# The second attention of a four-stage kernel: summary times W_out, scaled queries, and a new order of the tail

## The chip, the cores and the metric

One core of one Trainium2 chip. The metric is the device time of one execution in microseconds (us), as the median of several runs.

## The reference

One sequence of T = 2048 tokens with D = 128 features goes through four residual stages, each behind a layer norm: a causal softmax attention (16 heads of 8), a feed-forward with token shift, a linear attention, and the same feed-forward again.

```
x = x + attn_a(ln(x)); x = x + ffn(ln(x)); x = x + attn_b(ln(x)); x = x + ffn(ln(x))

attn_b: q, k, v = split(x @ w_qkv.T);  q, k = rope(q), rope(k)
        q_feat = elu(q * 8**-0.5) + 1;  k_feat = elu(k) + 1
        kv[h] = sum_t k_feat[t,h,:] outer v[t,h,:];  k_sum[h] = sum_t k_feat[t,h,:]
        out[t,h] = (q_feat[t,h] @ kv[h]) / max(q_feat[t,h] . k_sum[h], 1e-6)
        result = concat_h(out) @ w_out.T
ffn:    xr, xk = mixes of x[t] and x[t-1] by mu_r, mu_k
        result = sigmoid(xr @ W_r.T) * (square(relu(xk @ W_k.T)) @ W_v.T)
```

## The kernel before, in words

The tokens stand in four chunks (n = 0 to 3) of 512, each of four tiles of 128. Everything is fp32, in one program with a hand-written list of calls for each engine; an engine works its list strictly in order and waits at semaphores. A list entry such as `k_b(2)` is chunk 2 of that step; `(0, n)` and `(1, n)` are the first and second feed-forward, or queries (0) and keys (1) in `rope`, `features` and `feature_parts`.

Most of the span, up to 264 us, is the first attention: TensorE scores and weighs (L1126, L1147), ScalarE takes exponentials (L527). The change touches only what follows, the tail:

- First feed-forward: TensorE `mix_k_in` (L1201, L1205), `mix_r_in` and `mix_out` (both through `natural`, L980, four products of 128 columns in two passes each, so x8 in the trace); ScalarE `relu`, `squared`, `gate` (L542, L546, L551); VectorE `mix_r` (L864) and `add_mix` (L877, L878), which then takes the statistics of layer norm 3 (`ln_stats`, L652 to L658). `add_mix(0, n)` waits for both `gate(0, n)` and `mix_out(0, n)`. GpSimd raises the variance to -0.5 (`rstd_of`, L422) and forms the shift (L427); ScalarE applies the norm (`ln_act`, L536); TensorE turns it (`turn`, L975), ScalarE copies it out (L486).
- Second attention: TensorE `k_b`, `v_b`, `q_b` (L980). VectorE `rope` (L892 to L894, for chunk 3 also L898); for chunks 0 to 2 GpSimd adds the two halves (`turned`, L436). ScalarE `feature_parts` (L560, L561), VectorE `features` (L903). TensorE `summarize` (L1236) sums all chunks into `kv` and `k_sum` in one bank; VectorE `mask_kv` (L908, L909) keeps the blocks of the heads in `kvb[:, 0:D]` and puts `k_sum` by head in `kvb[:, D:D+H]`.
- Each chunk then passes `turn_q`, ScalarE's `turned_q`, `numerators` (L1250: numerators and denominators in one product of 144 columns), VectorE's `divide` (L915 maximum, L916 reciprocal, L917 product of the numerators in PSUM with the reciprocals), `turn_heads`, `turned_n`, `project_b` (L980, with W_OUT) and `add_y2` (L923 and the statistics of layer norm 4).
- Second feed-forward as the first, except that for chunks 1 to 3 VectorE forms both mixes (`mix_k_of` L870, L871; `mix_r` L864) after GpSimd's `shift` (L431). `add_mix(1, n)` ends a chunk and releases its store (L410).

The lists of TensorE, ScalarE and VectorE in the tail are the ones in the diff.

Of the kernel before, what the change touches and what calls it, by code (L numbers as in the profile page):

```python
# [18 lines left out]
P = 128  # L19
T = 2048  # L20
# [44 lines left out]
def program(nc, x_in, w_in, c_in, cb_in, krow_in, qrow_in, out):  # L65
    with ExitStack() as ctx:
# [62 lines left out]
        heads_out = mix_k  # L129
        k_tmp = att_t  # L130
        vb = scr[:, 14 * T + 8:14 * T + 8 + TILES * (D + 1)].rearrange("p (t n) -> p t n", t=TILES)
        kvb = scr[:, 15 * T + CH:15 * T + CH + D + H]
        w_mu = negmax[:, :].rearrange("p (i n) -> p i n", i=2)
# [45 lines left out]
        k_mixed = sem("k_mixed")  # L179
# [86 lines left out]
        def ln_apply(engine, waits, l, n, dst):  # L266
            waits.wait_ge(ln_rstd[l], n + 1)
            for j in range(TPC):
                ins = engine.tensor_scalar(dst[:, P * j:P * (j + 1)], x[:, TPC * n + j, :], negmean[:, n, j:j + 1],
                                           rstd[:, n, j:j + 1], ALU.add, ALU.mult)  # L270
            ins.then_inc(xh_ready[l] if l != LN1 else ln1_ready[n], 1)
# [143 lines left out]
        def _(pool):  # L415
# [54 lines left out]
            shift_of(LN4, 3)  # L470
            shift(1, 1)
            shift(1, 2)
            shift(1, 3)

        @block.scalar
        def _(act):
# [98 lines left out]

            relu(0, 0)
            squared(0, 0)
            gate(0, 0)
            relu(0, 1)
            squared(0, 1)  # L580
            gate(0, 1)
            ln_act(LN2, 3)
            relu(0, 2)
            squared(0, 2)
            turned_f(0, 3)
            gate(0, 2)
            ln_act(LN3, 0)
            ln_act(LN3, 1)
            relu(0, 3)
            squared(0, 3)  # L590
            gate(0, 3)
            turned_b(0)
# [4 lines left out]
            ln_act(LN3, 3)  # L597
            take_v(1)
            feature_parts(1, 0)
            turned_b(3)  # L600
            feature_parts(1, 1)
# [3 lines left out]
            feature_parts(1, 3)  # L605
            take_v(3)
            feature_parts(0, 1)
            feature_parts(0, 2)
            turned_q(0)
            turned_q(1)  # L610
            feature_parts(0, 3)
            turned_q(2)
            turned_n(0)
            turned_q(3)
# [8 lines left out]
            ln_act(LN4, 3)  # L623
            turned_f(1, 2)
            gate(1, 0)
            relu(1, 0)
            relu(1, 1)
            turned_f(1, 3)
            squared(1, 0)
# [7 lines left out]
            gate(1, 3)  # L637

        @block.vector
        def _(dve):  # L640
# [270 lines left out]
            def divide(n):  # L911
                dve.wait_ge(n_psum, n + 1)
                sums = ps[:, 2 * n:2 * n + 2, :].rearrange("p b (u m) -> p (b u) m", u=2)
                inv = rden[:, TPC * H * n:TPC * H * (n + 1)].rearrange("p (t h) -> p t h", h=H)
                then(nc.vector.tensor_scalar(inv, sums[:, :, D:D + H], 1e-6, None, ALU.max))  # L915
                then(nc.vector.reciprocal(inv, inv))  # L916
                nc.vector.tensor_tensor(heads_out[:, cols(n)].rearrange("p (t h v) -> p t h v", t=TPC, v=HD),  # L917
                                        sums[:, :, 0:D].rearrange("p t (h v) -> p t h v", v=HD),
                                        inv.unsqueeze(3).broadcast_to([P, TPC, H, HD]), ALU.mult).then_inc(n_ready, 1)
# [7 lines left out]

            add_y(3, high(3))
            add_mix(0, 0, LN3)
            add_mix(0, 1, LN3)  # L930
            mix_r(0, 3)
            add_mix(0, 2, LN3)
# [5 lines left out]
            features(1, 0)  # L938
            rope(0, 1)
            rope(1, 3)  # L940
            features(1, 1)
            features(1, 2)
            rope(0, 2)
            features(1, 3)
            features(0, 0)
            features(0, 1)
# [12 lines left out]
            mix_r(1, 0)  # L959
            mix_k_of(1)  # L960
            mix_r(1, 1)
            mix_k_of(2)
            mix_r(1, 2)
            mix_k_of(3)
            mix_r(1, 3)
# [3 lines left out]
            add_mix(1, 3, None)  # L969

        @block.tensor
        def _(pe):
# [273 lines left out]
            def numerators(n):  # L1246
                stage((kv_ready, 1), (qft_ready, max(n + 1, 2 * n - 2)))
                for j in range(TPC):
                    t = TPC * n + j
                    ins = nc.tensor.matmul(ps[:, t // 2, t % 2 * (CH // 2):t % 2 * (CH // 2) + D + H], qft[:, P * t:P * (t + 1)],  # L1250
                                           kvb[:, 0:D + H], start=True, stop=True)
                ins.then_inc(n_psum, 1)

            def turn_heads(n):
                pe.wait_ge(n_ready, n + 1)
                turn(heads_out[:, cols(n)], low(n, 1), nt_psum)

            def project_b(n):
                pe.wait_ge(nt_ready, n + 1)
                natural(high(n, 1), att_t[:, cols(n)], W_OUT).then_inc(y2_psum, 1)  # L1260

            def turn_ln4(n):
                stage((xh_ready[LN4], n + 1), (nt_ready, n + 1))
                turn(xh[:, cols(n)], low(n, 1), xt_psum[LN4])

            mix_k_in(0, 0)
            mix_r_in(0, 0)
            project(3)
            mix_out(0, 0)
            mix_k_in(0, 1)  # L1270
            mix_r_in(0, 1)
# [6 lines left out]
            turn_ln3(0)  # L1278
            mix_r_in(0, 3)
            turn_ln3(1)  # L1280
            mix_out(0, 3)
            k_b(0)
# [3 lines left out]
            q_b(0)  # L1286
            v_b(1)
            k_b(2)
            turn_ln3(3)
            q_b(1)  # L1290
            k_b(3)
            summarize(0)
            v_b(2)
            v_b(3)
            q_b(2)
            summarize(1)
            q_b(3)
            summarize(2)
            summarize(3)
            turn_q(0)  # L1300
            turn_q(1)
            numerators(0)
            turn_q(2)
            numerators(1)
            turn_heads(0)
            numerators(2)
            project_b(0)
            turn_q(3)
            turn_heads(1)
            numerators(3)  # L1310
# [9 lines left out]
            turn_ln4(2)  # L1320
            mix_k_in(1, 1)
            mix_r_in(1, 1)
            turn_ln4(3)
            mix_k_in(1, 2)
            mix_r_in(1, 2)
            mix_out(1, 0)
# [69 lines left out]
```

## Time and profile before

| | us |
|---|---|
| median of 3 runs (336.92 to 338.47) | 338.28 |
| profiled execution, its own time | 336.65 |
| profiled execution, span | 334.6 |
| TensorE busy in the span | 306.8 (92%) |
| ScalarE busy | 287.3 (86%) |
| VectorE busy | 161.4 (48%) |
| GpSimd busy | 57.6 (17%) |

The span lies within the execution's own time, which is 2.05 us longer. L numbers are lines of the kernel; PE is TensorE, PEld its weight loads, DVE VectorE, ACT ScalarE, POOL GpSimd. A merged entry such as "2.96 ... x2" is two instructions together.

### The profile page before, as it was taken

To read this page: it belongs to the slowest core of one execution; us is meant where nothing else is said; L and a number is where in the kernel's file an instruction comes from. 1 tells how busy PE (TensorE), PEld (TensorE's weight loads), DVE (VectorE), ACT (ScalarE), POOL (GpSimd) and SP (SyncE) were. 2 spreads that over 40 slices of the span, in tenths; PEclk is the share of its full clock that TensorE was granted. 3 is DMA by queue.
4 is the path that set the end of the run, shared out by engine and by line. 5 is a ranking of instruction groups with operands and counts; after the bars stand their busy time and mean duration, and the time that the engine had idled before them with its cause. 6 is when DMAs were issued, how large, how long until landed. Compare 5 with 4: busy or idle time off the path is not lost.

```text
span 334.6 us, 6057 instructions
## 1 busy us (share of the span) xinstructions
PE 306.8 (92%) x2314; PEld 132.5 (40%) x2314; DVE 161.4 (48%) x425; ACT 287.3 (86%) x411; POOL 57.6 (17%) x56
## 2 busy tenths in 40 slices
PE   3997999999999999999999999999999998979784
PEld 1562223233332323333332322223232467878564
DVE  6851133357545032432533313304613296998976
ACT  8547799998989999999889999998999678863782
POOL 5995000030000000100000100000000042910550
PEclk9996799999999999999999999999999999999999
DMA  7455566832004000000000000000000000000004
GB/s 222 141 150 184 164 187 190 243 123 76 0 2 125 3 0 2 0 2 0 2 1 3 0 2 0 2 0 2 0 3 0 2 0 3 0 2 0 2 1 125
DMA packets 13264, 16.43 MB, mean 49 GB/s; under 512 B 1488, under 2 KB 8016, under 8 KB 13136
## 3 DMA queue, kind: packets, MB, share of 16 engines
q1 hardware_dynamic: 13232, 16.01, 15.8%
q8 instruction: 20, 0.33, 0.4%
q14 instruction: 12, 0.10, 0.1%
HBM read 6.56 MB, written 2.62 MB: 27 GB/s over the span
## 4 chain that ended last, share of the span: by engine, by line
ACT 34%; PE 31%; DVE 17%; issue 12%; DMA 3%; SPq 1%; POOL 1%; ACTq 0%; DVEq 0%
ACT probs L527 23%; PE ps L1147 15%; PE ps L1126 11%; ACT parts_last L527 5%; ACT x L527 4%; PE ps L980 4%; DVE stats L652 3%; DMA kr<-parts_mid 2%; DVE scr L903 2%; DVE scr L892 1%; DMA x<-in_x 1%; ACT scr L536 1%; POOL rstd L422 1%; DVE mv L655 1%; DVE x L878 1%
## 5 line engine op out<-in xcount | busy, mean ns | idle before, releaser
L527 ACT ACTIVATE probs<-ps 128x1024 f32<-128x1024 f32 (+5 forms) x223 | 169.5, 859 | 13.2 <-PE ps L1126 12.1
L1126 PE MATMUL ps<-qr,kr 64*128 64x512 f32 (+6 forms) x592 | 110.7, 427 | 7.9 <-ACT probs L527 4.8
L1126 PEld LDWEIGHTS ps<-qr,kr 64*128 64x128 f32 x592 | 50.0, 187 | 125.8 <-ACT probs L527 85.8
L1147 PE MATMUL ps<-probs,vaug 128*9 128x512 f32 (+5 forms) x892 | 98.5, 499 | 0.4 <-DVE probs L845 0.4
L845 DVE TENSOR_TENSOR probs<-probs,cs 128x512 f32<-128x512 f32 x60 | 41.3, 689 | 99.9 <-ACT probs L527 99.7
L422 POOL TENSOR_TENSOR rstd<-veps,neghalf 128x4 f32<-128x4 f32 x16 | 17.1, 1068 | 222.7 <-DVE veps L658 222.6
L527 ACT ACTIVATE parts_last<-ps 128x1024 f32<-128x1024 f32 (+9 forms) x49 | 45.0, 974 | 1.4 <-PE ps L1126 1.2
L980 PE MATMUL ps<-w,scr 128*128 128x128 f32 x288 | 37.1, 280 | 2.6 <-DVE scr L864 1.1
L980 PEld LDWEIGHTS ps<-w,scr 128*128 128x128 f32 x288 | 34.4, 191 | 7.9 <-DVE scr L864 2.4
L1147 PE MATMUL ps<-parts_last,vaug 128*9 128x512 f32 (+9 forms) x196 | 25.4, 549 | 0.0
L1147 PEld LDWEIGHTS ps<-probs,vaug 128*9 128x9 f32 x892 | 13.6, 88 | 28.2 <-issue 17.1
L527 ACT ACTIVATE x<-ps 128x1024 f32<-128x1024 f32 (+4 forms) x24 | 20.5, 907 | 0.3 <-PE ps L1126 0.2
L779 DVE STREAM_TRANSPOSE ot<-ps 128x512 f32<-128x512 f32 x16 | 11.5, 717 | 16.8 <-PE ps L1147 16.5
L536 ACT ACTIVATE scr<-x,shift_by,rstd 128x128 f32<-128x128 f32 x36 | 14.8, 483 | 5.0 <-POOL shift_by L427 4.9
L975 PE MATMUL ps<-cs,scr 128*128 128x128 f32 x80 | 12.4, 280 | 2.6 <-ACT scr L536 2.1
L486 ACT COPY scr<-ps 128x512 f32<-128x512 f32 x17 | 9.7, 579 | 5.8 <-PE ps L975 5.6
L652 DVE BATCH_NORM_STATS2 stats<-x 128x6 f32<-128x128 f32 x64 | 13.9, 281 | 1.3 <-DMA x<-in_x 0.8
L1147 PE MATMUL ps<-x,vaug 128*9 128x512 f32 (+4 forms) x96 | 12.1, 566 | 0.0
L804 DVE TENSOR_TENSOR x<-ps,x 128x512 f32<-128x512 f32 x4 | 2.8, 692 | 19.0 <-PE ps L980 19.0
L975 PEld LDWEIGHTS ps<-cs,scr 128*128 128x128 f32 x80 | 8.8, 141 | 6.1 <-ACT scr L536 4.4
L446 POOL MEMSET qr<- 128x4096 f32 x3 | 10.5, 3506 | 0.0
L451 POOL MEMSET kr<- 128x4096 f32 x1 | 3.5, 3518 | 36.5 <-DMA kr<-parts_mid 36.5
(108 smaller groups left out, 238.5 us busy)
## 6 DMA issues: line engine op xcount, KB each, us to landing
x<-in_x SPq DMA_DIRECT2D x8, 256.0 KB, 3.9
qr<-parts_mid SPq DMA_DIRECT2D x16, 128.0 KB, 3.1
kr<-parts_mid SPq DMA_DIRECT2D x16, 128.0 KB, 3.1
kr<-att SPq DMA_DIRECT2D x8, 128.0 KB, 3.1
qr<-att SPq DMA_DIRECT2D x8, 128.0 KB, 3.2
qr<-parts_last SPq DMA_DIRECT2D x8, 128.0 KB, 3.7
kr<-parts_last SPq DMA_DIRECT2D x8, 128.0 KB, 3.2
out_y<-x SPq DMA_DIRECT2D x4, 256.0 KB, 2.3
```

The costliest lines, as they stand in the source:

```text
L422: nc.gpsimd.tensor_tensor(rstd[:, n], veps[:, n], neghalf[:], ALU.pow).then_inc(ln_rstd[l], 1)
L446: nc.gpsimd.memset(z.bitcast(F32)[:, :, :], 0.0).then_inc(zeroed, 1)
L486: nc.scalar.copy(dst, ps[:, bank, :]).then_inc(ready, 1)
L527: nc.scalar.activation(slot[:, 2 * u:2 * u + 2, w0:w1], ps[:, b:b + 2, w0:w1], ACT.Exp).then_inc(exp_done, 1)
L536: ins = nc.scalar.activation(xh[:, P * t:P * (t + 1)], x[:, t, :], ACT.Identity, bias=shift_by[:, n, j:j + 1], scale=rstd[:, n, j:j + 1])
L652: nc.vector.bn_stats(stats[:, n, j, :], x[:, TPC * n + j, :]).then_inc(dve_step, 1)
L779: nc.vector.transpose(ot[:], ps[:, 6 + ends[k].lane, :]).then_inc(ot_ready, 1)
L845: nc.vector.tensor_tensor(slot, slot, cs[:, C_TRI:C_TRI + P].unsqueeze(1).broadcast_to([P, 4, P]), ALU.min).then_inc(mask_done, 1)
L975: ins = nc.tensor.transpose(ps[:, bank, P * j:P * (j + 1)], src[:, P * j:P * (j + 1)], ident)
L980: ins = nc.tensor.matmul(ps[:, bank, P * j:P * (j + 1)], src[:, P * j:P * (j + 1)], w[:, c0:c0 + D], start=True, stop=True)
L1126: ins = nc.tensor.matmul(ps[:, 2 * (n % 3) + v, w0:w1], kr[kb // TPC][a:a + SIDE, j, P * (kb % TPC):P * (kb % TPC + 1)], qr[unit.c][a:a + ...
L1147: ins = nc.tensor.matmul(ps[32 * v:32 * v + V1, 6 + unit.lane, w0:w1], vaug[:, kb, V1 * h:V1 * (h + 1)], probs_slot(unit)[:, v, w0:w1], st ...
```

## The change

In the second attention the masked summary is turned (`turn_kv`), copied by ScalarE (`turned_kv`), multiplied by W_OUT (`kv_by_out`) and copied again (`take_kv_out`), once. TensorE forms only denominators from the turned features (`denominators`, 16 columns instead of 144). `divide` scales the queries' features in place, in SBUF, by the reciprocals; `turn_heads` turns these scaled features and `project_b` multiplies them by the copied product. A second edit moves the last layer-norm application (LN4, chunk 3) from ScalarE to VectorE (`ln4_last`, in `ln_apply`, L269), so that GpSimd forms no shift for it. The third is a new order of the lists of TensorE, ScalarE and VectorE in the whole tail. TensorE's wait for the last exponential moves from `mix_k_in(0, 0)` ahead of the first product of the list.

```diff
         q_rot, q_exp, q_relu, q_feat = prev_r, prev_k, mix_rt, mix_k
-        heads_out = mix_k
...
         kvb = scr[:, 15 * T + CH:15 * T + CH + D + H]
+        kv_turned, kv_out = (scr[:, 15 * T + 2 * CH + D * i:15 * T + 2 * CH + D * (i + 1)] for i in range(2))
...
-            ins.then_inc(xh_ready[l] if l != LN1 else ln1_ready[n], 1)
+            ins.then_inc(xh_last if (l, n) == (LN4, NCH - 1) else xh_ready[l] if l != LN1 else ln1_ready[n], 1)
...
             shift_of(LN4, 2)
-            shift_of(LN4, 3)
+            rstd_of(LN4, 3)
             shift(1, 1)
             shift(1, 2)
             shift(1, 3)
...
+            def turned_kv():
+                act.wait_ge(kvt_psum, 1)
+                nc.scalar.copy(kv_turned, ps[:, high(0, 1), 0:D]).then_inc(kvt_ready, 1)
+            def take_kv_out():
+                act.wait_ge(kvo_psum, 1)
+                nc.scalar.copy(kv_out, ps[:, high(0, 1), D:2 * D]).then_inc(kvo_ready, 1)
+            gate(0, 0)
+            gate(0, 1)
             relu(0, 0)
             squared(0, 0)
-            gate(0, 0)
             relu(0, 1)
             squared(0, 1)
-            gate(0, 1)
+            relu(0, 2)
             ln_act(LN2, 3)
-            relu(0, 2)
             squared(0, 2)
+            gate(0, 2)
             turned_f(0, 3)
-            gate(0, 2)
             ln_act(LN3, 0)
-            ln_act(LN3, 1)
             relu(0, 3)
             squared(0, 3)
+            turned_b(0)
+            ln_act(LN3, 1)
             gate(0, 3)
-            turned_b(0)
             ln_act(LN3, 2)
             turned_b(1)
             take_v(0)
             turned_b(2)
             ln_act(LN3, 3)
+            feature_parts(1, 0)
             take_v(1)
-            feature_parts(1, 0)
+            feature_parts(1, 1)
             turned_b(3)
-            feature_parts(1, 1)
             feature_parts(0, 0)
             feature_parts(1, 2)
             take_v(2)
-            feature_parts(1, 3)
             take_v(3)
             feature_parts(0, 1)
+            turned_q(0)
+            feature_parts(1, 3)
             feature_parts(0, 2)
-            turned_q(0)
             turned_q(1)
             feature_parts(0, 3)
             turned_q(2)
+            turned_kv()
             turned_n(0)
+            take_kv_out()
             turned_q(3)
             turned_n(1)
             turned_n(2)
...
             ln_act(LN4, 2)
             turned_f(1, 1)
-            ln_act(LN4, 3)
+            relu(1, 0)
+            squared(1, 0)
             turned_f(1, 2)
+            turned_f(1, 3)
             gate(1, 0)
-            relu(1, 0)
             relu(1, 1)
-            turned_f(1, 3)
-            squared(1, 0)
             squared(1, 1)
             gate(1, 1)
             gate(1, 2)
...
             def divide(n):
                 dve.wait_ge(n_psum, n + 1)
-                sums = ps[:, 2 * n:2 * n + 2, :].rearrange("p b (u m) -> p (b u) m", u=2)
-                inv = rden[:, TPC * H * n:TPC * H * (n + 1)].rearrange("p (t h) -> p t h", h=H)
-                then(nc.vector.tensor_scalar(inv, sums[:, :, D:D + H], 1e-6, None, ALU.max))
+                inv = rden[:, TPC * H * n:TPC * H * (n + 1)]
+                then(nc.vector.tensor_scalar(inv, ps[:, low(n, 1), 0:TPC * H], 1e-6, None, ALU.max))
                 then(nc.vector.reciprocal(inv, inv))
-                nc.vector.tensor_tensor(heads_out[:, cols(n)].rearrange("p (t h v) -> p t h v", t=TPC, v=HD),
-                                        sums[:, :, 0:D].rearrange("p t (h v) -> p t h v", v=HD),
-                                        inv.unsqueeze(3).broadcast_to([P, TPC, H, HD]), ALU.mult).then_inc(n_ready, 1)
+                q = q_feat[:, cols(n)].rearrange("p (t h v) -> p t h v", t=TPC, v=HD)
+                nc.vector.tensor_tensor(q, q, inv.rearrange("p (t h) -> p t h", h=H).unsqueeze(3).broadcast_to([P, TPC, H, HD]),
+                                        ALU.mult).then_inc(n_ready, 1)
...
+            def ln4_last():
+                ln_apply(nc.vector, dve, LN4, NCH - 1, xh[:, cols(NCH - 1)])
             add_y(3, high(3))
             add_mix(0, 0, LN3)
...
+            add_mix(0, 2, LN3)
             mix_r(0, 3)
-            add_mix(0, 2, LN3)
             add_mix(0, 3, LN3)
             rope(1, 0)
             rope(1, 1)
             rope(0, 0)
             rope(1, 2)
             features(1, 0)
+            features(1, 1)
             rope(0, 1)
+            features(0, 0)
             rope(1, 3)
-            features(1, 1)
             features(1, 2)
             rope(0, 2)
+            features(0, 1)
             features(1, 3)
-            features(0, 0)
-            features(0, 1)
             rope(0, 3)
             mask_kv()
             features(0, 2)
...
             mix_r(1, 0)
+            ln4_last()
             mix_k_of(1)
             mix_r(1, 1)
+            mix_r(1, 2)
             mix_k_of(2)
-            mix_r(1, 2)
+            mix_r(1, 3)
             mix_k_of(3)
-            mix_r(1, 3)
             add_mix(1, 0, None)
             add_mix(1, 1, None)
             add_mix(1, 2, None)
             add_mix(1, 3, None)
...
-            def numerators(n):
+            def turn_kv():
+                pe.wait_ge(kv_ready, 1)
+                nc.tensor.transpose(ps[:, high(0, 1), 0:D], kvb[:, 0:D], ident).then_inc(kvt_psum, 1)
+            def kv_by_out():
+                pe.wait_ge(kvt_ready, 1)
+                nc.tensor.matmul(ps[:, high(0, 1), D:2 * D], kv_turned, w[:, W_OUT:W_OUT + D], start=True, stop=True).then_inc(kvo_psum, 1)
+            def denominators(n):
                 stage((kv_ready, 1), (qft_ready, max(n + 1, 2 * n - 2)))
                 for j in range(TPC):
-                    t = TPC * n + j
-                    ins = nc.tensor.matmul(ps[:, t // 2, t % 2 * (CH // 2):t % 2 * (CH // 2) + D + H], qft[:, P * t:P * (t + 1)],
-                                           kvb[:, 0:D + H], start=True, stop=True)
+                    ins = nc.tensor.matmul(ps[:, low(n, 1), H * j:H * (j + 1)], qft[:, CH * n + P * j:CH * n + P * (j + 1)],
+                                           kvb[:, D:D + H], start=True, stop=True)
                 ins.then_inc(n_psum, 1)
             def turn_heads(n):
                 pe.wait_ge(n_ready, n + 1)
-                turn(heads_out[:, cols(n)], low(n, 1), nt_psum)
+                turn(q_feat[:, cols(n)], low(n, 1), nt_psum)
             def project_b(n):
                 pe.wait_ge(nt_ready, n + 1)
-                natural(high(n, 1), att_t[:, cols(n)], W_OUT).then_inc(y2_psum, 1)
+                pe.wait_ge(kvo_ready, 1)
+                for j in range(TPC):
+                    ins = nc.tensor.matmul(ps[:, high(n, 1), P * j:P * (j + 1)], att_t[:, CH * n + P * j:CH * n + P * (j + 1)], kv_out,
+                                           start=True, stop=True)
+                ins.then_inc(y2_psum, 1)
             def turn_ln4(n):
-                stage((xh_ready[LN4], n + 1), (nt_ready, n + 1))
+                stage((xh_last, 1) if n == NCH - 1 else (xh_ready[LN4], n + 1), (nt_ready, n + 1))
                 turn(xh[:, cols(n)], low(n, 1), xt_psum[LN4])
+            pe.wait_ge(exp_done, 3 + STEPS)
+            mix_r_in(0, 0)
+            mix_r_in(0, 1)
             mix_k_in(0, 0)
-            mix_r_in(0, 0)
...
+            mix_k_in(0, 1)
             mix_out(0, 0)
-            mix_k_in(0, 1)
-            mix_r_in(0, 1)
             mix_k_in(0, 2)
             mix_out(0, 1)
             mix_r_in(0, 2)
...
             mix_out(0, 2)
             mix_k_in(0, 3)
             turn_ln3(0)
+            mix_out(0, 3)
             mix_r_in(0, 3)
+            k_b(0)
             turn_ln3(1)
-            mix_out(0, 3)
-            k_b(0)
             v_b(0)
             turn_ln3(2)
             k_b(1)
             q_b(0)
+            k_b(2)
             v_b(1)
-            k_b(2)
+            v_b(2)
             turn_ln3(3)
             q_b(1)
+            summarize(0)
             k_b(3)
-            summarize(0)
-            v_b(2)
             v_b(3)
+            turn_q(0)
             q_b(2)
+            q_b(3)
             summarize(1)
-            q_b(3)
             summarize(2)
+            turn_q(1)
             summarize(3)
-            turn_q(0)
-            turn_q(1)
-            numerators(0)
+            denominators(0)
+            denominators(1)
             turn_q(2)
-            numerators(1)
+            turn_kv()
             turn_heads(0)
-            numerators(2)
+            kv_by_out()
+            denominators(2)
+            turn_q(3)
             project_b(0)
-            turn_q(3)
             turn_heads(1)
-            numerators(3)
+            denominators(3)
             turn_heads(2)
             project_b(1)
             project_b(2)
...
             turn_ln4(1)
             mix_r_in(1, 0)
             turn_ln4(2)
+            turn_ln4(3)
+            mix_out(1, 0)
             mix_k_in(1, 1)
             mix_r_in(1, 1)
-            turn_ln4(3)
+            mix_r_in(1, 2)
             mix_k_in(1, 2)
-            mix_r_in(1, 2)
-            mix_out(1, 0)
             mix_out(1, 1)
             mix_k_in(1, 3)
             mix_out(1, 2)
```

## Rows read from the trace of the kernel before

**Rows 1.** Busy time by stretch (start:end, length, busy us and instructions, clock)

```profile
0.00:264.00 264.00, 248.72 (x1899) 83.81 (x1899) 102.25 (x250) 239.86 (x314) 32.50 (x27) 0.98 0.19 58
...
290.00:300.00 10.00, 9.23 (x78) 8.51 (x76) 9.93 (x20) 7.97 (x15) 4.06 (x3) 1.00 0.01 2
...
325.00:330.00 5.00, 5.00 (x41) 4.52 (x40) 4.38 (x7) 3.41 (x6) 0.00 (x0) 1.00 0.22 67
```

**Rows 2.** Chain of waits that ended last (start us, us, what)

```profile
261.26 2.84 PE ps L1147 x24
...
266.26 1.17 PE ps L980 x8
...
269.68 0.60 DVE scr L877
...
272.46 0.60 DVE scr L877
...
300.99 1.26 PE ps L1250 x8
...
302.27 0.23 DVE rden L915
...
307.30 0.61 DVE x L923
...
317.03 0.07 issue
...
326.85 0.86 PE ps L1201 x2
327.71 2.69 PE ps L980 x24
...
331.22 0.69 DVE x L878
```

**Rows 3.** Timeline of ScalarE and VectorE around the first feed-forward's end

```profile
277.35 1.65 ACT L536 ACTIVATE scr<-x,shift_by,rstd 128x128 f32<-128x128 f32 x4 [0.97 <-POOL shift_by L427]
...
280.04 0.58 ACT L551 ACTIVATE scr<-ps 128x512 f32<-128x512 f32 x1
...
281.45 0.69 DVE L877 SCALAR_TENSOR_TENSOR scr<-scr,ps 128x512 f32<-128x512 f32 x1 [2.74 <-PE ps L980]
```

**Rows 4.** GpSimd's adds and VectorE's `features`, all (ns min/median/max), then the timeline

```profile
L436 POOL TENSOR_TENSOR scr<-scr x6: 1269/1276/1700, 285.7 to 295.8; 128x512 f32<-128x512 f32 x6
...
L903 DVE SCALAR_TENSOR_TENSOR scr<-scr x8: 679/685/1757, 289.3 to 303.7; 128x512 f32<-128x512 f32 x8
...
288.18 2.96 POOL L436 TENSOR_TENSOR scr<-scr 128x512 f32<-128x512 f32 x2
...
295.80 1.64 POOL L436 TENSOR_TENSOR scr<-scr 128x512 f32<-128x512 f32 x1 [3.17 <-DVE scr L894]
...
296.23 2.36 DVE L903 SCALAR_TENSOR_TENSOR scr<-scr 128x512 f32<-128x512 f32 x2
```

**Rows 5.** Timeline of TensorE's weight loads, and a large operand beside a small GpSimd instruction

```profile
290.30 0.97 PEld L1236 LDWEIGHTS ps<-scr 128*128 128x128 f32 x8
...
269.76 1.01 POOL L422 TENSOR_TENSOR rstd<-veps,neghalf 128x4 f32<-128x4 f32 x1 [79.22 <-DVE veps L658]
...
270.31 0.69 DVE L878 TENSOR_TENSOR x<-x,scr 128x512 f32<-128x512 f32 x1
```

**Rows 6.** Last layer norm and mixes: timeline, ns min/median/max, groups (busy us, mean ns | idle)

```profile
317.10 1.44 POOL L422 TENSOR_TENSOR rstd<-veps,neghalf 128x4 f32<-128x4 f32 x1 [0.77 <-DVE veps L658]
...
L871 DVE SCALAR_TENSOR_TENSOR scr<-scr,w x3: 750/977/1061, 319.0 to 323.9; 128x512 f32<-128x512 f32 x3
...
L864 DVE SCALAR_TENSOR_TENSOR scr<-scr,w 128x512 f32<-128x512 f32 x5 | 3.7, 745 | 0.5 <-POOL scr L431 0.5
...
L870 DVE TENSOR_SCALAR scr<-scr,omu 128x512 f32<-128x512 f32 x3 | 1.4, 483 | 1.0 <-ACT scr L486 1.0
...
139.37 1.12 DVE L269 TENSOR_SCALAR scr<-x,negmean,rstd 128x128 f32<-128x128 f32 x4 [1.14 <-POOL rstd L422]
```

More of the change, by code:

```diff
@@ L178, in program @@
         rot_ready, rot_last, feat_act, feat_ready = ([sem(f"{s}_{m}") for m in "qk"] for s in ("rot_ready", "rot_last", "feat_act", "feat_ready"))
-        k_mixed = sem("k_mixed")
+        k_mixed, xh_last = sems("k_mixed xh_last")
+        kvt_psum, kvt_ready, kvo_psum, kvo_ready = sems("kvt_psum kvt_ready kvo_psum kvo_ready")
         n_psum, n_ready, nt_psum, nt_ready, y2_psum, y2_added = sems("n_psum n_ready nt_psum nt_ready y2_psum y2_added")
```

## The prediction

> **What bounds the kernel now.** I read the stretches first. Up to 264 us TensorE and ScalarE carry the first attention, and nothing of the change is in there [rows 1]. All that can move is the tail, 264 to 334.6 us. Then the chain of waits: from 269.68 to 317.03 us it stands on VectorE nearly throughout [rows 2], and VectorE is busy for 9.93 of the 10 us from 290 to 300 [rows 1]. It leaves VectorE in that part at two places: before the fourth `add_mix`, where VectorE sat idle for 2.74 us [rows 3], and at the first numerators, from the end of `mask_kv`, 0.05 ahead of 300.99, to the start of `divide(0)` at 302.27, 1.33 us [rows 2]. Behind 317.03 (the end of `add_y2(3)`, called D below) the chain passes the last layer norm, and TensorE is full from 325 to 330 [rows 1]; it ends in three `natural` steps of 2.69 us together and VectorE's `add_mix(1, 3)`, at 331.91 [rows 2]. What the change is worth is thus the sum of VectorE's idle time and work from 267 us to D, and of whichever of VectorE and TensorE is last behind D. TensorE or ScalarE work saved elsewhere is worth nothing by itself.
>
> Prices that recur: a `natural` step in a stream 2.69 / 3 = 0.90 us, alone 1.17; `mix_k_in` 0.86 in a stream [rows 2]; an `add_mix` with its statistics 272.46 - 269.68 = 2.78 [rows 2], without them 0.60 + 0.69 + 0.04 of gaps = 1.33 [rows 2].
>
> **1. Entry, up to the fourth `add_mix`.** TensorE's part of the attention ends at 264.1, with the next loads begun at 264.0; `project(3)` then waited for the attention's last heads and started at 266.26 [rows 2]. Now two `mix_r_in` and a `mix_k_in` stand ahead of `project(3)`: 264.0 + 0.95 + 0.9 + 0.86 = 266.7, plus about 1.1 = 267.8, against 266.26 + 1.17 = 267.43. So `add_y(3)` and the first `add_mix` are later by 0.35: 270.03. The wait moved ahead of the list costs nothing by itself, since the old first entry waited for the same exponential. `add_mix` 0 to 2 then follow without gap: 270.03 + 3 x 2.78 = 278.37. `mix_r(0, 3)`, formerly between the second and third, comes behind: + 0.70 = 279.07. TensorE's `mix_r_in(0, 3)` takes 1.17: 280.25. ScalarE's `gate(0, 3)` takes 0.58 [rows 3] and a semaphore 0.05: `add_mix(0, 3)` starts at 280.95, against 281.45 [rows 3]. The new list puts `relu(0, 3)` ahead of the 1.65 us `ln_act(LN3, 1)` which stood before it [rows 3], so `mix_out(0, 3)` is done near 279.0; but `add_mix` needs the gate too, and that is late next. **Term: -0.5.** Bounds: -2.4, if the gate were no obstacle (279.05), and +0.35.
>
> **2. `features` beside GpSimd's adds.** The adds take 1.27 us each, but one 1.70; `features` take 0.68, but one 1.76 [rows 4]. These are the same event: GpSimd's add was issued at 295.80, just behind a `features`, and ended at 297.44; the next `features`, whose inputs were long there, was issued at 296.23 and ended near 297.97 (two in 2.36 us) [rows 4]. So a VectorE instruction with two SBUF inputs does not run beside a GpSimd add, and loses 1.757 - 0.685 = 1.07 us. `rope` reads PSUM and one SBUF table, and ran beside these adds unharmed.
> Before, behind `features(1, 0)` came `rope(0, 1)`; now `features(1, 1)`. At that moment GpSimd holds its fourth add: the third and fourth fill 288.18 to 291.14 [rows 4], 0.42 us more than two of 1.27, which is the wait for `features(1, 0)`. Everything is 0.5 earlier now: `features(1, 0)` ends near 289.5, GpSimd's add (chunk 2 of the keys) has waited since 288.95 and runs until 290.64, and `features(1, 1)` (its ScalarE input is ready at about 289.5) ends at 290.64 + 0.54 = 291.2 where 290.1 was possible. The old wait of 1.07 at 296.23 stays: `features(1, 3)` now stands behind the last add instead of `features(0, 0)`. `features(0, 0)` starts right at the end of `rope(0, 1)`, some 0.1 us before GpSimd's next add is released, and goes first. **Term: +1.1.** Bounds: 0, if VectorE gets in ahead of the waiting add, and +2.2, if `features(0, 0)` is caught too.
> The Trainium skill ("SBUF — State Buffer", section "SBUF: two separate sides") says of this: VectorE with two SBUF inputs and GpSimd share a port pair, the first to start holds it, the other blocks fully. These rows agree for large operands. Read strictly, the rule also speaks against the new `divide`, whose product now has two SBUF inputs instead of PSUM and SBUF: `divide(3)` would meet the end of GpSimd's power on four elements, and the sum would rise by some 0.35. The rows show otherwise: `add_mix`'s second instruction (two SBUF inputs) took its usual 0.69 at 270.31 in the middle of such a power of 1.01 us [rows 5]. My sum has nothing for it.
>
> **3. The rest up to `mask_kv`.** TensorE's new order has `v_b(2)` ahead of `turn_ln3(3)` (0.9 later, at about 287.7), `turned_b(3)` ends at about 290.1 and `k_b(3)` at 291.6; VectorE needs it at 293.1. `q_b(3)` is done at 295.6, `summarize(3)` about 1 us behind `features(1, 3)`, beside `rope(0, 3)` of 2 us. ScalarE's feature parts stay at least 1 us ahead. **Term: 0**; without that cover `v_b(2)`'s 0.9 would count. `mask_kv` ends at 300.94 - 0.5 + 1.1 = 301.55.
>
> **4. The algebra.** Removed: four products of 144 columns, 1.26 us for a chunk [rows 2]. Added: four of 16 columns. No row shows one so narrow. From below, the weight loads bound it: eight loads of this size take 0.97 us [rows 5]; from above 1.26. I take 1.0, since the loads already fill most of the 1.26. Only the first chunk's is on the path: **-0.25** (0 to -0.3). The other three are hidden behind `divide`, of which the three instructions stay in number and size. Added once: a transpose, a product, two ScalarE copies of 128 columns, estimated at 1.2 us with their handovers from ScalarE's 0.58 us for 512 columns [rows 3] and a quarter of a `natural` step each, the rest being handovers. They lie beside `divide(0)`, `features(0, 3)` and `divide(1)`. From 301.55, `divide(0)` runs 302.55 to 304.05, `turn_heads(0)` and `kv_by_out` follow to 305.3, `denominators(2)` to 306.2, just when `divide(1)` ends (302.27 to 307.30 held `divide` 0 to 2 and `features(0, 3)`, 5.03 us [rows 2]). `turn_q(3)` and `project_b(0)` end at 307.65, against 307.58 for VectorE. So I add **+0.1**; if these two small waits do not coincide as I have them, 0 to +0.9. Then `divide(3)` and four `add_y2` follow as before, 9.73 us: D = 302.55 + 5.03 + 0.1 + 9.73 = 317.4, against 317.03.
>
> **5. Behind D.** Before, 331.91 - 317.03 = 14.88 us. GpSimd's power ends at D + 1.52 (1.44 us instead of 1.01, since it starts beside `mix_r`) [rows 6]; no shift behind it, no ScalarE 1.65. VectorE applies the norm in 1.12 [rows 6], pitch 1.08. Then VectorE has three `mix_k_of` (0.48 + 0.75 + gap = 1.27) and three `mix_r` (0.67 pitch) [rows 6], 5.82, four `add_mix` of 1.33 and 0.08 for the last. Sum 1.53 + 1.08 + 5.82 + 5.40 = 13.83. To this come three GpSimd `shift` instructions, which all read SBUF beside it: L871 took 0.75 to 1.06 [rows 6], so 0.31 at a hit; three hits make 0.85 to 0.9: 14.7. TensorE: `turn_ln4(3)` at D + 3.2, and then with waits for the mixes the last product ends near D + 13.05, + 1.46 = 14.5, so VectorE is last. **Term: -0.2.** Bounds: -1.0 (no hits) and +0.5 (each hit a whole `shift`, about 0.55).
>
> **Sum.** -0.5 + 1.1 - 0.25 + 0.1 - 0.2 = +0.2 on a span of 334.6 and an execution of 336.65. The stores behind the last `add_mix` stay. The profiled execution is 1.63 below the median of 338.28; I put the same change on the median: 338.5.
>
> **Rivals.**
> *Faster*: the collision at `features(1, 1)` does not come (a slightly earlier or later fourth add), and VectorE has no hits behind D: 0.2 - 1.1 - 0.8 = -1.7, 336.6. For it: the old trace shows only one such loss among six adds [rows 4]. Against: the fourth add was already waiting when `features(1, 0)` ran.
> *Slower*, one mechanism: VectorE loses against GpSimd wherever both want SBUF, at `features(0, 0)` too (+1.1), and for a whole `shift` at each of the three behind D (+0.7 over my term): 0.2 + 1.8 = +2.0, 340.3. It decides if GpSimd's add gets in ahead of `features(0, 0)`, that is, if that starts more than 0.1 us behind the end of `rope(0, 1)`; against it, its ScalarE input is 1.4 us early in my walk.
> *The change does not do what it says*: 16 columns cost as much as 144, and `kv_by_out` delays `project_b(0)`: +0.25 + 0.5, 339.2; no change that can be told.
>
> **How the numbers follow.** Forecast 0.50, its own range 337.6 to 339.4; faster rival 0.27; slower rival 0.17; the last 0.06. 0.5% is 1.7 us, about what a measurement can tell from no change. The faster rival stands on that border, as the bound of term 1 (-1.9 more) reaches beyond it, so its chance goes to faster; the forecast and the last go to same, 0.56. The range 336.4 to 340.0 leaves out about 1 in 10 at each side.
>
> **What would show it.** The fourth `add_mix` starts at 280.9 behind `gate` (not 279); one more L903 of about 1.7 us near 290; `mask_kv` ends near 301.5; denominators take 1.0; D near 317.4; no gap over 0.2 us ahead of `add_y2(0)`; L269 in some 1.1 to 1.6 us behind D, and VectorE without idle time from there to the end. I am wrong if the gate comes earlier, if `features(1, 1)` runs in 0.68, or if the end behind D is under 14 us.

## The result: slower, and the profile after

The changed kernel took 342.42 us (median of 4 runs, 341.72 to 345.63) against 337.64 for the kernel before in the same comparison: ratio 1.0157, 95% interval 1.0116 to 1.0198. I had forecast no change, 338.5, in a range of 336.4 to 340.0. Here and below, a ratio leaves out executions over 1.5% above the fastest of their kernel, so it is not the quotient of the medians.

Executions differ by some us before the attention ends, so all comparisons of traces below are of the *tail*: from the end of the attention's last 24 products to the end of the last `add_mix`. Tails and stretches are those of the profiled executions; of the others only the time and the mean clock are known. Before it was 331.91 - 264.10 = 67.81 us [rows 2]. In the changed kernel, the chain of waits (start, length, what):

```profile
261.62 2.80 PE ps L1163 x24
...
281.28 0.70 DVE scr L889
...
289.19 2.32 DVE scr L915 x2
...
301.90 3.38 PE ps L1274 x16
...
310.31 1.72 PE ps L1286 x8
312.03 0.02 issue
312.05 0.70 DVE x L934
...
321.88 0.07 issue
...
332.51 2.69 PE ps L996 x24
...
336.02 0.69 DVE x L890
```

The tail is 336.71 - 264.42 = 72.29 us, 4.48 longer. Up to the first denominators (L1274) it is 301.90 - 264.42 = 37.48, against 36.89 before [rows 2], and behind D (321.88) it is 14.83, against 14.88. Nearly all of the loss, 3.94 us, lies between: 19.98 against 16.04. There the chain, which stood on VectorE, stands on TensorE from 301.90 to 312.03. The stretches of the changed kernel show why (start:end, length; busy us of PE, PEld, DVE, ACT, POOL; then TensorE's granted clock):

```profile
298.00:301.90 3.90, 1.71 (x13) 1.28 (x13) 3.87 (x8) 2.00 (x4) 0.96 (x1) 1.00 0.00 0
302.10:312.30 10.20, 10.20 (x50) 10.02 (x50) 5.50 (x12) 2.75 (x7) 0.00 (x0) 0.50 0.01 2
```

Before, the same part of the kernel:

```profile
298.00:301.00 3.00, 1.27 (x9) 0.85 (x9) 2.96 (x8) 2.18 (x5) 0.00 (x0) 1.00 0.00 0
301.00:307.00 6.00, 5.79 (x48) 5.58 (x48) 5.05 (x11) 2.07 (x5) 0.00 (x0) 1.00 0.00 0
```

The granted clock went from 1.00 to 0.50 (2.4 to 1.2 GHz) at about 302.15, 0.25 us after the first 16-column product, and came back at about 312.4. TensorE is shown busy for the whole of it, the weight loads for 10.02 of 10.20 us, and yet it finished 50 matmuls in 10.2 us where before it finished 48 in 6. The timeline of the stretch:

```profile
301.90 3.38 PE L1274 MATMUL ps<-scr 128*128 128x16 f32 x16 [1.18 <-DVE scr L921]
...
303.61 0.23 DVE L926 TENSOR_SCALAR rden<-ps 128x64 f32<-128x64 f32 x1 [1.18 <-PE ps L1274]
...
309.41 0.23 DVE L926 TENSOR_SCALAR rden<-ps 128x64 f32<-128x64 f32 x1 [2.21 <-PE ps L1274]
...
312.05 0.69 DVE L934 TENSOR_TENSOR x<-ps,x 128x512 f32<-128x512 f32 x1 [1.10 <-PE ps L1286]
```

The first denominators took about 1.7 us (301.90 to 303.6), not 1.0; VectorE waited 2.21 us for the third chunk's and 1.10 us for the first `project_b`.

### The profile page after: what moved, and what is told of

Read it like the earlier page. It is cut to its first block, busy times and chain, and to the rows that moved or that the text cites. A ratio compares the mean times of both kernels' runs of the same rounds, so it can differ in the third digit from the quotient of the medians.

```text
span 339.8 us, 6068 instructions
## 1 busy us (share of the span) xinstructions
PE 310.4 (91%) x2317; PEld 137.7 (41%) x2317; DVE 164.2 (48%) x429; ACT 286.5 (84%) x409; POOL 57.0 (17%) x55
## 4 chain that ended last, share of the span: by engine, by line
PE 38%; ACT 34%; issue 12%; DVE 11%; DMA 3%; POOL 1%; SPq 0%; ACTq 0%; DVEq 0%
ACT probs L529 23%; PE ps L1163 14%; PE ps L1142 10%; PE ps L996 5%; ACT parts_last L529 5%; ACT x L529 4%; DMA kr<-parts_mid 2%; PE ps L991 2%; PE ps L1009 2%; DVE scr L915 2%; DVE stats L664 2%; PE ps L1274 1%; DVE scr L904 1%; PE ps L1217 1%; DMA cs<-in_consts 1%
## 5 line engine op out<-in xcount | busy, mean ns | idle before, releaser
L996 PE MATMUL ps<-w,scr 128*128 128x128 f32 x256 | 32.8, 279 | 2.4 <-DVE scr L876 1.1
L996 PEld LDWEIGHTS ps<-w,scr 128*128 128x128 f32 x256 | 30.6, 192 | 7.9 <-issue 3.1
L1163 PEld LDWEIGHTS ps<-probs,vaug 128*9 128x9 f32 x892 | 13.7, 89 | 28.0 <-issue 16.8
L991 PE MATMUL ps<-cs,scr 128*128 128x128 f32 x80 | 14.4, 309 | 3.8 <-ACT scr L538 2.1
L538 ACT ACTIVATE scr<-x,shift_by,rstd 128x128 f32<-128x128 f32 x32 | 13.2, 483 | 3.7 <-POOL shift_by L428 3.7
L991 PEld LDWEIGHTS ps<-cs,scr 128*128 128x128 f32 x80 | 10.6, 163 | 7.1 <-ACT scr L538 3.9
L1163 PE MATMUL ps<-x,vaug 128*9 128x512 f32 (+4 forms) x96 | 11.3, 529 | 0.0
L437 POOL TENSOR_TENSOR scr<-scr 128x512 f32<-128x512 f32 x6 | 8.8, 1470 | 4.7 <-DVE scr L906 4.7
```

The source lines that it names most:

```text
L538: ins = nc.scalar.activation(xh[:, P * t:P * (t + 1)], x[:, t, :], ACT.Identity, bias=shift_by[:, n, j:j + 1], scale=rstd[:, n, j:j + 1])
L991: ins = nc.tensor.transpose(ps[:, bank, P * j:P * (j + 1)], src[:, P * j:P * (j + 1)], ident)
L996: ins = nc.tensor.matmul(ps[:, bank, P * j:P * (j + 1)], src[:, P * j:P * (j + 1)], w[:, c0:c0 + D], start=True, stop=True)
L1163: ins = nc.tensor.matmul(ps[32 * v:32 * v + V1, 6 + unit.lane, w0:w1], vaug[:, kb, V1 * h:V1 * (h + 1)], probs_slot(unit)[:, v, w0:w1], st ...
```

## The experiments

Thirteen kernels were run. The lists moved in an edit are given by their entries.

**Which half of the change is it?** Four kernels together.

`e1_old_algebra`: the new lists, the old steps.

```diff
-            denominators(0)
+            numerators(0)
...
-            turn_kv()
...
-            kv_by_out()
```

> The changed kernel with all its new orders, but with the numerators of 144 columns, the division in PSUM and the projection by W_OUT of before. In the changed kernel TensorE's granted clock fell to 0.50 at about 302.2 us, 0.3 us after the first 16-column product, and came back at about 312.2. Theory IDLE (the thin work of TensorE between 297.9 and 301.9, a matter of the order, lets the clock fall): it falls here too near 302; the time is 340 to 342. Theory NARROW (products of 16 columns do it): the clock stays 1.00 and the time is that of before within 0.3%, 337 to 338.

Measured: 338.43 us (10 runs), ratio 1.0006 (0.9964 to 1.0048); tail 68.32 us, clock 1.00 in all of it.

`e2_algebra_alone`: the old lists, the new steps (the reverse diff, on the kernel before).

> The kernel before with the algebra alone: denominators, scaled queries, product with W_OUT once; all lists in the order of before, with the four small steps put in. IDLE: TensorE's work ahead of the denominators is that of before, the clock stays 1.00, the time is 337.5, within 0.3% of before. NARROW: the clock falls to 0.50 soon after the first denominators, the time is 340.5 to 342.5.

Measured: 342.12 us (4 runs), ratio 1.0143 (1.0071 to 1.0214); tail 72.43 us, clock 0.50 from 302.6 to about 316.3.

`e3_wide_denominators`: all of the change, but products of 128 columns, of which `divide` reads the last 16.

```diff
-                    ins = nc.tensor.matmul(ps[:, low(n, 1), H * j:H * (j + 1)], ...
-                                           kvb[:, D:D + H], start=True, stop=True)
+                    ins = nc.tensor.matmul(ps[:, low(n, 1), P * j:P * (j + 1)], ...
+                                           kvb[:, D + H - P:D + H], start=True, stop=True)
```

> The changed kernel with denominators of 128 columns in place of 16 (112 of them not used), each chunk in the same bank. IDLE: the clock falls near 302 all the same, since the work ahead of it is unchanged, and the time is 340.5 to 342.5. NARROW: the clock stays 1.00, the time is 337.5 to 338.5.

Measured: 338.12 us (10 runs), ratio 0.9999 (0.9962 to 1.0036); tail 68.31 us, clock 1.00.

`e4_filler`: all of the change, with two products added.

```diff
             turn_q(1)
+            nc.tensor.matmul(ps[:, 3, :], ident, w[:, 0:CH], start=True, stop=True)
             summarize(3)
+            nc.tensor.matmul(ps[:, 3, :], ident, w[:, 0:CH], start=True, stop=True)
             denominators(0)
```

> The changed kernel with two products of 512 columns added on TensorE, whose results nobody uses, one ahead of summarize(3) and one behind it, where TensorE waited for about 1.0 and 1.2 us. IDLE: the clock stays 1.00 and the time is 337.5 to 338.5. NARROW: the clock falls to 0.50 all the same, at most some us later, and the time is 340 to 342.5.

Measured: 338.30 us (10 runs), ratio 1.0012 (0.9969 to 1.0054); tail 68.18 us. Its stretches, which answer to the two of the changed kernel (its attention ended 3.57 us later):

```profile
301.50:305.40 3.90, 3.48 (x16) 1.82 (x16) 3.87 (x8) 1.94 (x4) 1.01 (x1) 1.00 0.00 0
305.50:312.00 6.50, 6.36 (x55) 5.95 (x55) 5.73 (x12) 2.95 (x8) 0.00 (x0) 1.00 0.00 0
```

What follows: the order alone costs nothing that can be told (e1), the algebra alone has the whole loss (e2), and it is neither the added steps nor the two added copies as such, since they run at full clock in e3 and, with the narrow products, in e4. Both of my theories are contradicted: IDLE by e1, e2 and e3, NARROW as I had put it by e4, where the narrow products are all there, at 1.08 us for the first chunk:

```profile
305.45 1.08 PE ps L1274 x8
```

**What sets the fall off, and what keeps it going?** The changed kernel with 128 columns for some chunks only (`m = P if n in (0,) else H`, and the reverse; `divide` reads the columns accordingly).

> The changed kernel, no filler, with the denominators of chunk 0 alone 128 columns wide, those of chunks 1 to 3 of 16. If the clock falls by how thin the work has been up to and just behind the start of the denominators, a wide first chunk keeps it at 1.00 and the time is 338 to 339. If each narrow product counts, the clock falls during chunk 1 and the time is 341 to 342.5.

Measured for `e7_wide_first`: 340.09 us (9 runs), ratio 1.0040 (0.9992 to 1.0088). The profiled execution kept its clock, tail 68.25. The time is outside both ranges that I gave. Two other executions had a mean clock of 0.975, where the lowest of e3's ten had 0.982, so they may have lost it; without their traces this stays open.

> The changed kernel, no filler, with the denominators of chunk 0 alone of 16 columns, those of chunks 1 to 3 of 128. If the first chunk decides, the clock falls near 302.2 us as in the changed kernel, but with wide products behind it comes back sooner than after 10 us; time 339.5 to 342. If the narrow products of chunks 1 to 3 are needed for the fall, the clock stays 1.00 and the time is 338 to 339.

Measured for `e8_narrow_first`: 340.06 us (9 runs), ratio 1.0046 (1.0007 to 1.0085). In the profile the clock fell at about 302.85, 0.25 us behind the first denominators, and was back at about 309.7, after 6.8 us in place of 10.2; tail 71.11. This is the first of the two cases that I gave.

Two later kernels were built for speed (below) and spoke to this as well. `e10_gate_alone` has the old algebra with its 144 columns, and in its profile the clock fell nevertheless, within 0.1 us of the start of the first numerators at 299.66:

```profile
296.00:299.70 3.70, 1.94 (x15) 1.33 (x13) 3.67 (x9) 2.73 (x5) 0.12 (x1) 1.00 0.02 4
299.70:303.10 3.40, 3.40 (x15) 3.39 (x16) 1.55 (x4) 1.01 (x3) 0.00 (x0) 0.50 0.00 0
303.10:305.00 1.90, 1.90 (x17) 1.90 (x17) 1.83 (x5) 0.84 (x2) 0.00 (x0) 1.00 0.00 0
```

So narrow products are not needed for a fall, but this one was over in 3.4 us. Nor does the work ahead decide alone: in the 3 us ahead of the first numerators TensorE was busy for 1.26 us in e10 and for 1.26 us before, and before it kept its clock. The fall was probably no rarity in e10: six of its twelve executions had a mean clock of 0.979 at 336.5 to 338.4 us, the profiled one among them, and in the kernel before a mean clock that low went with 340 us or more.

To tell the stretch ahead and the narrow products apart, 512-column products were put ahead of wide ones (`e12_gate_filler`) and behind narrow ones (`e13_filler_behind`: twice the filler line between `denominators(1)` and `turn_q(2)`).

> The kernel of e10 (the kernel before with the earlier gate, old algebra, products of 144 columns) with two unused products of 512 columns ahead of the first numerators, as in e9. In e10's profile the clock fell to 0.50 for about 3.4 us from 299.9, with wide products, and the tail was 67.36 us with numerators(0) at 2.29 in place of 1.26. Theory THIN (the fall is set off by the thin stretch ahead, the narrow products only keep it going): the filler holds the clock at 1.00, the tail is 66.2 to 66.7 us and the time 0.4% to 0.7% below before. If filler is no cover for wide products, the tail stays 67.3.

Measured: 336.67 us (12 runs), ratio 0.9965 (0.9937 to 0.9992), so 0.35% below before where I gave 0.4% at the least; clock 1.00 and tail 66.32, as THIN has it.

> The changed kernel, no filler ahead, but two unused products of 512 columns directly behind denominators(1). THIN: the fall at the first denominators comes all the same, since the work ahead of it is unchanged, but the clock is back after 3 to 6 us instead of 10.2, and the tail is 69.5 to 71.5 us against 72.29 in the changed kernel. If the narrow products set it off and keep it down whatever stands between, it stays down some 10 us and the tail is over 72.5.

Measured: 342.47 us (4 runs), ratio 1.0167 (1.0102 to 1.0232); tail 73.26. The clock fell 0.25 us behind the start of the first denominators and was back in the middle of the slice 308 to 309:

```profile
301.00:302.00 1.00, 0.59 (x4) 0.59 (x4) 0.95 (x4) 0.96 (x2) 0.00 (x0) 0.82 0.00 0
...
307.00:308.00 1.00, 1.00 (x2) 0.23 (x1) 0.00 (x0) 0.00 (x0) 0.00 (x0) 0.50 0.00 0
308.00:309.00 1.00, 1.00 (x8) 0.79 (x7) 0.00 (x0) 0.02 (x1) 0.00 (x0) 0.76 0.00 0
```

That is 6.8 us of low clock: less than the 10.2 of the change, but not the 3 to 6 that THIN gave. The tail is even longer than in the change and lies where I had put the rival (over 72.5), because the two fillers themselves ran at half clock on the path (3.6 us, from 304.8 to 308.4). So e13 bears neither theory out as written; with e8 it shows two falls with wider products behind the first narrow ones, both shorter than that of the change.

**Is the port collision worth undoing?** `e5_features_apart` is e4 with VectorE's list `features(1, 0)`, `rope(0, 1)`, `features(1, 1)`, `rope(1, 3)`, `features(0, 0)`, `features(1, 2)`.

> The kernel of e4_filler (the changed kernel with two unused products ahead of the denominators) with VectorE's list altered: rope(0, 1) between features(1, 0) and features(1, 1), and features(0, 0) behind rope(1, 3). The tail, from the end of the attention's last products to the end of the last add_mix, was 67.81 us before and 68.18 in e4. Theory PORT (features(1, 1) lost 1.1 us to GpSimd's add because it stood directly behind features(1, 0)): the L915 of about 1.7 us near features(1, 1) is gone, mask_kv ends 1.0 earlier and the tail is 67.1 to 67.3. Rival: the wait moves to another features or to k_b(3), and the tail stays within 0.3 of 68.18. In the time that is 0.3%, at the edge of what can be told.

Measured: 338.88 us (10 runs), ratio 1.0029 (0.9990 to 1.0067), tail 68.63, 0.45 longer than e4. The timeline of VectorE:

```profile
290.16 0.69 DVE L904 TENSOR_TENSOR scr<-ps,cs 128x512 f32<-128x512 f32 x1 [0.19 <-PE ps L996]
...
291.43 0.68 DVE L915 SCALAR_TENSOR_TENSOR scr<-scr 128x512 f32<-128x512 f32 x1
...
296.44 0.69 DVE L904 TENSOR_TENSOR scr<-ps,cs 128x512 f32<-128x512 f32 x1 [1.04 <-PE ps L996]
```

`features(1, 1)` runs in 0.68, so the loss at this place was indeed the collision. But `rope(0, 1)` now waits for `q_b(1)` (0.19 us by its row), and `rope(0, 2)` 1.04 us for `q_b(2)`, which stands behind `turn_q(0)` and so behind the moved `features(0, 0)`. The rival was right: the wait moved.

**Is the gate what the fourth `add_mix` waits for?** `e6_early_gate`: e5, and the entry altered. On ScalarE, not shown below, `gate(0, 3)` moves directly behind `squared(0, 3)`, and `turned_b(1)` ahead of `ln_act(LN3, 2)`.

```diff
+            mix_r(0, 3)
             add_mix(0, 2, LN3)
-            mix_r(0, 3)
...
             mix_k_in(0, 3)
+            mix_r_in(0, 3)
             turn_ln3(0)
             mix_out(0, 3)
-            mix_r_in(0, 3)
```

> The kernel of e5 with the entry altered: mix_r(0, 3) ahead of add_mix(0, 2) on VectorE, mix_r_in(0, 3) ahead of turn_ln3(0) on TensorE, gate(0, 3) directly behind squared(0, 3) and turned_b(1) ahead of ln_act(LN3, 2) on ScalarE. If the gate was what the fourth add_mix waited for, it starts about 1.5 to 1.8 us earlier and the tail is 65.3 to 66.3 us, the time 0.4% to 0.7% below before, 336 to 337. If the next wait (k_b(1) or k_b(2) for rope) takes it up, the tail is 67 or more. The clock should stay 1.00 behind 265 us, but TensorE's thin stretch is not the same, so a fall is possible: then the tail is over 69.

Measured: 339.83 us (10 runs), ratio 1.0073 (1.0029 to 1.0116), tail 68.71: slower than before, and the rival of this run was right. The fourth `add_mix` starts 282.69 - 267.52 = 15.17 us into the tail instead of 281.28 - 264.42 = 16.86: 1.69 earlier, as expected. One `rope` later it is gone, in a wait of 1.57 us for `k_b(1)`:

```profile
282.69 0.69 DVE L889 SCALAR_TENSOR_TENSOR scr<-scr,ps 128x512 f32<-128x512 f32 x1 [0.19 <-PE ps L996]
...
288.38 0.69 DVE L904 TENSOR_TENSOR scr<-ps,cs 128x512 f32<-128x512 f32 x1 [1.57 <-PE ps L996]
```

**A version that beats both.** Three kernels: the algebra with filler on the lists of before (`e9_algebra_filler`), the early gate on them (`e10_gate_alone`), and both together (`e11_gate_algebra_filler`).

> The kernel before, all lists in the order of before, with the algebra alone as in e2, and two products of 512 columns whose results nobody uses, one behind summarize(3) and one ahead of the first denominators. The clock should stay 1.00 behind 265 us. By my step 4 the tail (attention's last product to the last add_mix; 67.81 us before, 72.43 in e2) is then 67.6 to 68.1, and the time that of before within 0.4%. If narrow products alone suffice for the fall, the tail is over 70.

Measured: 339.32 us (10 runs, 8 of them in the ratio), ratio 1.0012 (0.9971 to 1.0053), tail 67.65 with the clock at 1.00. The two slowest executions, 342.5 and 342.9 us, had a mean clock of 0.970, where none of the 29 of before had less than 0.978; so the fillers probably did not hold it in them, which no trace shows.

`e10_gate_alone`:

```diff
             ln_act(LN3, 0)
-            ln_act(LN3, 1)
             relu(0, 3)
             squared(0, 3)
             gate(0, 3)
             turned_b(0)
+            ln_act(LN3, 1)
...
             mix_k_in(0, 3)
+            mix_r_in(0, 3)
             turn_ln3(0)
-            mix_r_in(0, 3)
-            turn_ln3(1)
             mix_out(0, 3)
             k_b(0)
+            turn_ln3(1)
```

> The kernel before with nothing but an earlier gate(0, 3): ScalarE's relu, squared, gate (0, 3) and turned_b(0) ahead of ln_act(LN3, 1), TensorE's mix_r_in(0, 3) ahead of turn_ln3(0), and mix_out(0, 3) and k_b(0) ahead of turn_ln3(1). The fourth add_mix starts 1.5 to 2 us earlier. In e6 the next wait, k_b(1), took 1.57 us of that. Here the later lists are those of before, with VectorE the last; I expect 0.7 to 1.1 us to be left: tail 66.7 to 67.1, time 0.2% to 0.3% below before. Rival: k_b(1) takes nearly all of it here too, tail 67.5 to 67.9.

Measured: 336.55 us (12 runs) against 338.17, ratio 0.9958 (0.9929 to 0.9987). The first numerators start 35.38 us into the tail, 1.5 earlier than before. The tail of 67.36, for which I had given 66.7 to 67.1, holds the fall shown above, in which those products took 2.29 instead of 1.26 us; e12, the same kernel with fillers, shows 66.32 without it. The times of the two, 0.9958 and 0.9965, can't be told apart.

> The two edits of e9 and e10 together. Tail 66.5 to 67.1 us, clock 1.00 behind 265 us, time 0.2% to 0.4% below before. If the clock falls, the tail is over 70 us.

Measured: 337.89 us, ratio 0.9987 (0.9950 to 1.0023). The profiled execution, the slowest of the twelve at 342.72 us, lost its clock from about 307.75 to 314.6 (6.8 us); tail 68.52, where I gave 66.5 to 67.1 without a fall and over 70 with one. Four others had mean clocks of 0.970 to 0.976, below all 29 of before, so it was probably not the only one. The fall came in spite of the fillers, 3 us behind the start of the narrow products, and TensorE was busy for 2.81 of those 3 us. e9 had the same 3 us and kept its clock (first row e11, second e9):

```profile
304.72:307.72 3.00, 2.81 (x24) 2.62 (x25) 2.37 (x5) 1.63 (x4) 0.00 (x0) 1.00 0.00 0
...
305.60:308.60 3.00, 2.81 (x24) 2.62 (x25) 2.37 (x5) 1.63 (x4) 0.00 (x0) 1.00 0.00 0
```

## Why the prediction was wrong

**The step that failed is term 4, the algebra.** I priced 16-column products at 1.0 us between the weight loads (0.97) and the old products (1.26), and let everything behind them cost what it cost before. At full clock the price nearly holds: 1.08 in e4 and e9. With it e9's tail is 0.16 shorter than before, where my terms for the algebra (-0.25 and +0.1) give 0.15; that is partly chance, since the products gave 0.18 and the added steps cost 0.02 instead of 0.1. What I left out is that TensorE's clock can change with what it does: the sum assumed the old clock for new work. TensorE ran at half clock for 10.2 us, the first denominators took 1.7 us instead of 1.0, and D came 57.46 us into the tail, where I forecast 53.3 and where e4, the same kernel with fillers and at full clock, has 53.35. None of my rivals had it, and my range had no room for it.

The Trainium skill had the rule ("TensorE: Matmul & The Clock Gate", "What's actually happening"): "the default state is throttled, and activity releases the throttle", and the level is set by how busy TensorE has been recently. The traces agree in both levels, 0.50 and 1.00, but e10 and e11 show that TensorE's busy time in the profile does not tell by itself when a fall comes. It should have stood as a rival: before, TensorE had 1.27 us of work in the 3 us ahead of the first numerators, at full clock.

**The mechanism, as far as shown.** That the loss is the half clock is shown: the lists and the algebra of the change, with two unused products added, have a tail of 68.18 at full clock (e4), and with wide products 68.31 (e3). What sets a fall off is open. The stretch ahead of the first numerators or denominators is thin in every version without fillers (VectorE works off `features`, `rope` and `mask_kv`), and e10 shows that it can be followed by a fall with 144 columns, for 3.4 us. But the same stretch stood in the kernel before without a fall, and e11 fell without a thin stretch, inside the narrow products. The change, e8 and e13 fell 0.25 us behind their first narrow product; e1, e3 and e7, with the same work ahead of wider first products, kept their clock in the profile. All executions of the change, of e2 and of e13 were 341.3 us or more. So narrow products go with falls in many executions, but no trace shows how. The falls in the profiles lasted 13.7 (e2), 10.2 (the change), 6.8 (e8, e11 and e13) and 3.4 us (e10): the two longest are those with 16 columns for every chunk and no filler. Open too is why e11 fell where e9, with the same 3 us ahead, did not.

**The other terms held in size, one of them by another path**, counted from the start of the tail. Term 1: the fourth `add_mix` at 16.86, behind `gate` as forecast, before 17.35. I forecast 16.85, but had added wrongly: 280.25 + 0.58 + 0.05 is 280.88, so 16.78. In the changed kernel:

```profile
281.28 0.69 DVE L889 SCALAR_TENSOR_TENSOR scr<-scr,ps 128x512 f32<-128x512 f32 x1 [1.88 <-ACT scr L553]
...
335.30 0.69 DVE L889 SCALAR_TENSOR_TENSOR scr<-scr,ps 128x512 f32<-128x512 f32 x1 [0.16 <-PE ps L996]
```

The second row is the start of the last `add_mix`. Term 2: the two `features` in 2.32 us of the chain, near 290; the mechanism and the size (+1.1) are as forecast, the first denominators at 37.48 against 37.50, which holds for terms 1 to 3 together. But e5 corrects what term 2 is worth: the collision filled time in which VectorE would have waited for TensorE anyway, so "0 without the collision" was no bound of the total. Term 5: 14.83 behind D, forecast 14.7, before 14.88. But I had VectorE last and without idle time, and that row shows it waiting 0.16 us for TensorE at the end, which was last. The norm took 1.54 us beside a GpSimd `shift`, not 1.12, and only two of VectorE's mixes were slowed, so the size is in part luck. The order and the algebra without the fall are thus e3 and e4: tails of 68.31 and 68.18, 0.4 to 0.5 longer than before; my sum gave +0.2.

**The rivals.** The faster one had no chance once the collision came as forecast. The slower one named a second loss of the port, which did not occur; the time fell on its side for another reason.

## What to carry to other kernels

A step that gives TensorE fewer columns for the same weight loads saved little here (1.08 us instead of 1.26), and was followed by up to 13.7 us at half clock. Before such a step, above all where the profile shows TensorE thin just ahead of it, work out the sum a second time at half clock. Wide products kept the clock in e3's profile; unused ones ahead did so in e4's, e9's and e12's, but not in e11's, and behind the fall (e13) they cost more than they gave. Before removing a wait, look at what the next instruction of that engine waits for: in e5 and e6 it took back all of it, in e10 it did not. And compare traces by a stretch that starts where the change starts.

## What the runs showed of the hardware

TensorE was shown as busy for 10.20 of 10.20 us, its weight loads for 10.02, and the granted clock stayed at 0.50 for all of it: a full busy row is no sign of full clock. And the first attention, in which nothing was changed, ended between 263.97 and 269.34 us in the profiled executions: from 30 to 60 us the mean clock was 0.88 in the profile of before and 0.82 in e4's, with the attention's end 3.9 us later. This probably makes most of the spread of the runs: e4's three executions with a mean clock of 0.978 took 340.9 to 341.6 us, its four with 0.986 or more took 337.1 to 338.1.
